# Banks of the row maxima in two kinds: diagonal tiles of four heads with one mask product, and the tiles left of the diagonal without a mask

## The reference

```python
s1 = einsum('bhtd,bhsd->bhts', q1, k1) * scale + mask     # mask: -inf right of the diagonal
s2 = einsum('bhtd,bhsd->bhts', q2, k2) * scale + mask
a1, a2 = softmax(s1), softmax(s2)
out = einsum('bhts,bhsd->bhtd', a1 - lam * a2, v)         # then a norm, Wo, residual, layer norm
```

## Time and profile before

| | |
|---|---|
| median of 3 runs | 824.52 us |
| runs | 827.38, 824.46, 824.52 us |
| profiled execution, its own time | 826.78 us |
| its span in the trace | 825.1 us |
| mean granted TensorE clock | 0.956 of full speed |
| steps of batch 0, 1, 2, 3 (first score on PE) | from about 69, 204, 362, 513 us |
| routed experts | from about 671 us to the end |

### The profile page before, as it was taken

The page is one execution under the profiler, slowest core; times in us unless marked ns, Lnnn a source line. Parts: engine busy times, 40 slices in busy tenths (PEclk is TensorE's granted clock), DMA queues, the critical chain, the costliest instruction groups (busy, mean ns, idle before and its releaser), DMA issues.

```text
span 825.1 us, 11250 instructions
## 1 busy us (share of the span) xinstructions
PE 740.3 (90%) x3890; PEld 407.1 (49%) x3890; DVE 471.5 (57%) x1040; ACT 316.6 (38%) x584; POOL 308.1 (37%) x263
## 2 busy tenths in 40 slices
PE   7588899999889999997899997899999798999993
PEld 3233334334334444543444444444326557999993
DVE  2756886763657876446678754576525342334332
ACT  2415544444555334355553331655663011111110
POOL 4057711120984131139721210321420034666653
PEclk9878999999989999999999998799999999999997
DMA  4598085102009510120282104500110056777630
GB/s 132 146 340 168 18 187 83 19 22 40 1 26 183 87 35 27 21 46 24 48 159 45 58 0 84 160 2 0 36 49 1 26 193 213 267 267 243 234 123 1
DMA packets 55831, 78.73 MB, mean 95 GB/s; under 512 B 11543, under 2 KB 43037, under 8 KB 53920
## 3 DMA queue, kind: packets, MB, share of 16 engines
q1 hardware_dynamic: 47072, 65.02, 30.8%
q0 software_dynamic: 3824, 6.83, 2.5%
q10 hardware_dynamic: 4880, 6.16, 2.2%
HBM read 58.32 MB, written 22.41 MB: 98 GB/s over the span
## 4 chain that ended last, share of the span: by engine, by line
PE 69%; DVE 13%; POOL 6%; issue 5%; DMA 3%; ACT 2%; SPq 1%; POOLq 0%; DVEq 0%; ACTq 0%
PE pv_ps L1017 16%; PE wide_ps L1097 10%; PE s_ps L856 7%; PE wide_ps L1003 7%; DVE mneg L1435 6%; PE wide_ps L844 5%; PE wide_ps L987 3%; PE s_ps L888 3%; PE s_ps L857 3%; PE wide_ps L959 3%; PE misc L1108 2%; PE pv_ps L1108 2%; PE misc L934 2%; POOL w_exp L1348 2%; PE wide_ps L992 2%
## 5 line engine op out<-in xcount | busy, mean ns | idle before, releaser
L1435 DVE TENSOR_REDUCE mneg<-s_ps 128x1 f32<-128x384 f32 (+3 forms) x352 | 215.5, 638 | 96.3 <-PE s_ps L857 92.5
L1216 ACT ACTIVATE w_exp<-wide_ps 128x512 f32<-128x512 f32 x320 | 178.9, 601 | 102.7 <-PE wide_ps L1003 101.2
L1017 PE MATMUL pv_ps<-w_exp,work 128*64 128x512 f32 x640 | 176.7, 633 | 3.0 <-ACT work L1234 1.9
L1348 POOL TENSOR_SCALAR_AFFINE_SELECT w_exp<-w_exp 128x1024 f32<-128x1024 f32 x64 | 70.7, 1108 | 278.8 <-ACT w_exp L1216 278.8
L856 PE MATMUL s_ps<-w_exp 96*128 96x256 bf16 (+3 forms) x512 | 129.9, 313 | 17.5 <-DVE mneg L1435 9.4
L1003 PE MATMUL wide_ps<-w_exp 98*128 98x512 bf16 x320 | 122.4, 397 | 15.4 <-ACT w_exp L1216 14.0
L1003 PEld LDWEIGHTS wide_ps<-w_exp 98*128 98x128 bf16 x320 | 31.0, 102 | 154.0 <-ACT w_exp L1216 83.3
L857 PE MATMUL s_ps<-mask,identb 128*128 128x128 bf16 (+2 forms) x352 | 89.1, 253 | 0.0
L1097 PE MATMUL wide_ps<-tables,w_exp 128*128 128x128 f32 x736 | 85.9, 275 | 0.0
L1097 PEld LDWEIGHTS wide_ps<-tables,w_exp 128*128 128x128 f32 x736 | 84.1, 192 | 0.1
L856 PEld LDWEIGHTS s_ps<-w_exp 96*128 96x128 bf16 x512 | 45.1, 100 | 62.9 <-DVE mneg L1435 37.2
(11 more groups left out here) (161 smaller groups left out, 962.4 us busy)
## 6 DMA issues: line engine op xcount, KB each, us to landing
w_exp<-w_up_in SPq DMA_DIRECT2D x23, 1024.0 KB, 5.5
w_exp<-q_parts SPq DMA_DIRECT2D x96, 128.0 KB, 5.1
slot_tokens<-x ACTq DMA_DIRECT2D x1, 4864.0 KB, 19.1
work<-x_in SPq DMA_DIRECT2D x8, 512.0 KB, 4.4
w_exp<-w_down_in SPq DMA_DIRECT2D x8, 512.0 KB, 8.7
q_parts<-w_exp SPq DMA_DIRECT2D x6, 512.0 KB, 6.4
w_exp<-k_parts SPq DMA_DIRECT2D x18, 128.0 KB, 4.1
gated_rows<-work SPq DMA_DIRECT2D x4, 512.0 KB, 3.0
```

What stands on the lines that cost most here:

```text
L1017: last = nc.tensor.matmul(pv_ps[s * 64:(s + 1) * 64, :], vo[:, kt, g, :], probs[:, n % NP, s, :], start=(kt == 0), stop=(kt == qt))
L1216: nc.scalar.activation(probs[:, n % NP, s], st_bank(v), ACT.Exp, scale=float(DH) ** -0.5).then_inc(st_done, 1)
L1348: nc.gpsimd.affine_select(out=e, in_=e, compare_op=ALU.is_ge, fill=0.0, base=0, pattern=[[0, 8], [1, P]], channel_multiplier=-1).then_inc( ...
L1435: nc.vector.tensor_reduce(out=mneg[:, qt, rows[0]:rows[-1] + 1], in_=s_ps[:, (v - 1) % 2, 0:len(rows) * w].rearrange("p (r k) -> p r k", r ...
```

## The change

Banks are of two kinds now. For each query tile there are first 8 diagonal banks: the diagonal key tile alone, 4 heads of 128 columns, and one mask product over all 512 columns. For query tiles 1 to 3 the key tiles left of the diagonal follow in banks of their own, without a mask: 4 heads of 128 columns, 2 heads of 256, or 1 head of 384. That is 8, 16, 24 and 40 banks, again 88 a batch. A batch has 32 mask products of 512 columns in place of 88 (of 512, 256 and 128 columns), and 224 score matmuls in place of 128. The two partial (negated) maxima of a head meet in one minimum of 128x32 on DVE after the last bank of query tiles 1 to 3, before the split, each instruction of this chain waiting for the one before. The steps over which banks are spread are unchanged.

```diff
 def banks(qt):
-    per = max(1, QT // (qt + 1))
-    return [list(range(i, i + per)) for i in range(0, HS, per)]
+    per = QT // qt if qt else HS
+    return [(True, list(range(i, i + QT))) for i in range(0, HS, QT)] + ([(False, list(range(i, i + per))) for i in range(0, HS, per)] if qt else [])
...
-        mneg = sb("mneg", [P, QT, HS])
+        mneg = sb("mneg", [P, 2, 2, HS])
...
-                rows = banks(qt)[i]
-                w = (qt + 1) * P
+                own, rows = banks(qt)[i]
                 keys = k_stack[:, b % 2]
+                tiles = slice(qt, qt + 1) if own else slice(0, qt)
+                w = (tiles.stop - tiles.start) * P
                 o = s_ps[:, (v - 1) % 2, 0:len(rows) * w].rearrange("p (n k) -> p n k", k=w)
                 for n, hs in enumerate(rows):
-                    nc.tensor.matmul(o[:, n], q_stack[0:KROWS, qt, hs, :], keys[0:KROWS, hs // 4, 0:qt + 1, :], start=(n == 0), stop=False)
-                last = nc.tensor.matmul(o[:, :, w - P:w], identb[:], mask[:].unsqueeze(1).to_broadcast([P, len(rows), P]), start=False, stop=True)
+                    last = nc.tensor.matmul(o[:, n], q_stack[0:KROWS, qt, hs, :], keys[0:KROWS, hs // 4, tiles, :], start=(n == 0),
+                                            stop=(not own and n == len(rows) - 1))
+                if own:
+                    last = nc.tensor.matmul(o, identb[:], mask[:].unsqueeze(1).to_broadcast([P, len(rows), P]), start=False, stop=True)
...
-                w = (qt + 1) * P
-                nc.vector.tensor_reduce(out=mneg[:, qt, rows[0]:rows[-1] + 1],
+                w = P if own else qt * P
+                nc.vector.tensor_reduce(out=mneg[:, 1 - own, qt % 2, rows[0]:rows[-1] + 1],
...
                     dve.wait_ge(bank_done, v)
-                    c.link(nc.vector.tensor_copy(msplit[:, qt % 2, 0:HS], mneg[:, qt]))
-                    nc.vector.tensor_tensor(msplit[:, qt % 2, HS:2 * HS], mneg[:, qt], msplit[:, qt % 2, 0:HS],
+                    if qt > 0:
+                        c.link(nc.vector.tensor_tensor(mneg[:, 0, qt % 2], mneg[:, 0, qt % 2], mneg[:, 1, qt % 2], ALU.min))
+                    c.link(nc.vector.tensor_copy(msplit[:, qt % 2, 0:HS], mneg[:, 0, qt % 2]))
+                    nc.vector.tensor_tensor(msplit[:, qt % 2, HS:2 * HS], mneg[:, 0, qt % 2], msplit[:, qt % 2, 0:HS],
                                             ALU.subtract).then_inc(split_done, 1)
```

## The result

The changed kernel took 834.65 us (median of 9 runs, 827.21 to 836.99), the kernel before, timed beside it, 824.24 (median of 9, 821.89 to 827.38): ratio 1.0105, 95% interval 1.0069 to 1.014. It is slower by 1%, ten microseconds, and lies above the range that was given. The profiled execution took 835.86 us, with a span of 834.1 against 825.1, at a mean granted clock of 0.947 against 0.956.

A forecast was written before the change was run, and what follows sets the result against it. The prediction took the kernel as PE-bound (TensorE 90% busy) with short holes around the banks. Its terms summed to -2.9 us, from 824.52 to a predicted median of 821.6 us, range 816 to 829.

The forecast's parts named there:

- the wait at step 19: Batches 1 to 3: PE waits for reduction, minimum and split after a second bank; +0.8, +0.8, +1.6, in all +3.2 us.
- +-3.4 us that I don't put in the sum: Clock, 204.7:271.9: moved banks may remove or shift a half-speed stretch; +-3.4 us, left out of the sum.
- the end of step 8: Batch 0: last reduction 0.13 us longer and the minimum adds 0.22, so +0.35 at the split of tile 2.
- tile 3's denser banks: Batch 0, steps 9 to 17: 3 or 4 banks a step become 4 or 5; +1.4 us.
- Columns: PE, all batches: same columns, 224 mask products fewer and 384 scores more; -0.1 us a batch, -0.4 in all.
- the rival of 847: All 128-column scores: weight loads set their pace, 23 us more, 847 us; chance 0.03.
- Tile 2 ahead: Steps 28 to 38: fewer three-bank clusters, so fewer PE holes; -2.3 us in batch 0, -1.3 each in batches 1 and 2.
- Tile 2 in batch 0: Batch 0, steps 0 to 8: holes between banks fall from 3.3 to 0.8 us; taken as -2.0.
- Early banks: Batches 1 and 2, steps 2 to 19: diagonal banks fill PE's idle time, later steps shrink; -1.75 us each, -3.5.
- Tile 3 in batch 3: Batch 3, steps 2 to 19: no gain from early banks, and a new cluster of three at step 6 costs 0.4 us.
- x2 behind more reductions: Steps 10 and 15, three batches: the normalised rows x2 start later behind extra reductions on DVE; +1.2 and +0.9 us.
- the drain: Slower rival, step 19: PE waits 1.57 us in each of three batches, with other costs; 830 us, chance 0.14.

The follow-up runs named there:

- E5: Changed kernel with POOL's select of step 20 cut to one of its eight blocks: 828.27 us, ratio 1.0045 to the kernel before.
- E2: Changed kernel without the minimum, so the maxima of the left tiles are not used: 831.25 us, ratio 1.0067 to the kernel before.
- E3: Kernel before with one bank of query tile 3 moved from step 18 to step 19, which then holds two: 832.13 us, ratio 1.0089.
- E1: Changed kernel with one of step 19's two banks moved back to step 18: 825.79 us, ratio 0.9999 to the kernel before.
- E9: Changed kernel with one bank moved from step 19 to 18 and tile 2's transpose in batch 0 from step 8's end to mid-step 9: 823.79 us, ratio 0.9977.
- E4: Kernel before with a minimum of a tile with itself added before the split for query tiles 1 to 3: 827.09 us, ratio 1.0025.
- E8: Kernel before with two bank kinds for tile 2 alone, its batch 0 transpose moved from step 8's end to mid-step 9: 821.07 us, ratio 0.996.
- E10: Changed kernel with both transposes later: tile 2's to mid-step 9 (batch 0), tile 3's to mid-step 20 (batches 1 to 3): 834.01 us, ratio 1.0103.

## Why the prediction was wrong

The forecast was 821.6 and the time 834.65. The step that failed is the wait at step 19, "1.57 in each of three batches", summed as +3.2. The mechanism and the place were right, and so was the sign; the size was not. It measured 2.4 of lost time in each batch (7.2), and 1.9 more in steps 20 and 21 of batches 1 and 2 with their half-speed clock, where 1.6 was to come back: 9.1 for a term of 3.2. Two things were missing in it.
- The sequence of the earlier trace rows was taken as the price: instructions of 0.18 and 0.19 us. At step 19 POOL's select of step 20 starts at just that time, and the first of DVE's small instructions behind its start is held until the select ends: 1.05 in place of 0.19. E5 (0.25 with a short select), E2 and E3 (the cast caught in its place) show it. The select was in the trace of before at the same point of the step, and it held a DVE instruction even there: x2, 0.40 in the changed kernel's batch 1, took 1.17. The forecast never asked what POOL would be doing when the split moved there.
- The forecast gave back half of each drain because PE waits for DVE behind it anyway. That wait did go, but PE then ran a stretch at half speed: 8.6 us became 9.5 and 9.6. E3 shows the same stretches at the same places in the kernel before, E1 and E5 none. At full clock (E5, and E2 in batch 1) the two steps take 8.0, so 0.6 comes back, near the 0.8 forecast, and half speed takes 1.5. The clock was named in the prediction, as "+-3.4 us that I don't put in the sum"; a wait of 2.3 us made by the change itself is a reason to put it in on one side.

Both show in E5, which has neither: its step 19 takes 5.3 us, 1.6 more than before in each batch, and 0.6 comes back in batches 1 and 2. That is 3.6 in all, and the forecast's +3.2 was nearly right for a chain without POOL beside it. The trace of before, batch 1, step 20:

```profile
272.72 1.09 POOL L1348 TENSOR_SCALAR_AFFINE_SELECT w_exp<-w_exp 128x1024 f32<-128x1024 f32 x1
272.79 1.17 DVE L1506 TENSOR_SCALAR x<-y,mv,rstd 128x256 f32<-128x256 f32 x1 [0.47 <-POOL rstd L1328]
```

The second miss is the end of step 8, forecast at +0.35 with the minimum: steps 8 to 17 of batch 0 took 6.6 more, against +1.4 for tile 3's denser banks and that. The wait for the split grew by 2.25 (3.43 against 1.18), the half-speed stretch behind it is 6.8 us long, which costs up to 3.4, and about 1 us is left for the banks. Steps 10 to 17, behind the drain, took 26.2 before, 27.0 in the changed kernel at a clock of 0.97, and 26.7 in E9 at full clock. So the denser clusters cost about 0.5 there; what they cost in step 9 can't be told from the drain, and the forecast's 1.4 was for both.

The Trainium skill, "SBUF — State Buffer", section "Who interferes with whom", has the rule that the forecast lacked: a DVE instruction with two inputs in SBUF, or a copy or cast in a mode with two ports, shares a port with GpSimd, and the one that starts second is blocked until the first is done; reductions are never blocked. The traces agree: the minimum and the subtraction (two SBUF inputs) and the cast end 0.04 to 0.05 behind POOL's instruction when they start while it runs, the subtraction keeps its 0.19 when it starts 0.03 ahead (E4), and E9's reductions keep their 0.69. Which mode the cast ran in, no run shows. By it the minimum at step 19 would have been priced at the select's 1.09 in place of its own 0.19, an estimated 0.9 more a batch, 2.7 in all.

The other terms, in the prediction's order:
- Columns, -0.4, and the loads' pace: four 128-column scores with their loads took 0.22 us from start to start, as forecast, so the rival of 847 falls, and with it the 838 estimated from the Trainium skill, "TensorE: Matmul & The Clock Gate", section "Back-to-back issue gap", with its 81 ns a pair.
- Tile 2 ahead, -2.3 in batch 0 and -1.3 each in batches 1 and 2: measured -1.8, -1.3, -1.3 over steps 28 to 36. Right but for 0.5 in batch 0, and E8, which has only tile 2's banks in two kinds, shows the same.
- Tile 2 in batch 0, -2.0: -0.8 up to step 7, then the drain.
- Early banks, -1.75 each in batches 1 and 2: batch 1 -1.4 (+0.7 and -2.1). The way differs from the forecast. PE's 3.45 us for an exponential did not shrink to 1.8: PE now meets the third bank of a cluster there, and waits 2.96 for a reduction that stands on DVE behind x2, which POOL's product holds for 2.09 (timeline after, below). Batch 2 shows +1.7 in the changed kernel, with a clock of 0.84 in its steps 7 to 18 against 0.91; in E9 it shows -1.0.
- Tile 3 in batch 3, no gain and +0.4 for step 6: steps 0 to 18 took 1.0 more. Steps 0 to 6 alone took 24.1 in place of 21.7, steps 7 to 18 34.1 in place of 35.5. The work moved forward as forecast, but into a stretch whose clock is 0.81 (0.77 before), while the steps that lost it stand at 1.00.
- x2 behind more reductions, +2.1: not seen. PE's waits for x2 fell from 7.4 to 2.8 us, and the 2.11 of the earlier trace rows to 0.4, while those of the score matmuls for a buffer rose from 9.4 to 18.0.

```profile
228.43 2.17 POOL L586 TENSOR_TENSOR w_exp<-w_exp 128x1024 f32<-128x1024 f32 x1
228.66 2.09 DVE L1511 TENSOR_SCALAR x<-y,mv,rstd 128x256 f32<-128x256 f32 x1
231.27 0.50 PE L857 MATMUL s_ps<-w_exp 96*128 96x384 bf16 x1 [2.96 <-DVE mneg L1438]
```

Among the rivals the drain had the right mechanism, with a chance of 0.14 and a time of 830; it was short by the two parts above. Had the prediction's sum been made with the measured drain (9.1 for 3.2) and the measured steps 8 to 17 (6.6 for about 1.8), it would have stood at -2.9 + 5.9 + 4.8 = +7.8, against the +9.0 of the profiled span.

What stays open: what decides whether a half-speed stretch follows a wait. The length alone does not. At step 19 the wait is the same in batches 1, 2 and 3, and half speed followed in batches 1 and 2 but not 3 of the changed kernel (2.27) and of E3 (1.93), and in batches 2 and 3 but not 1 of E2 (2.04). It followed E10's pair of waits in all three (1.00 and 1.34, in batch 3 2.0 and 0.3), none of the waits of 1.47 in E5, and not the one of 2.19 in E8. And E9 against E8 doesn't tell whether tile 3 in two kinds costs a microsecond or two.

## What to carry to other kernels

When an edit moves the last piece of work ahead of a hand-over (last bank, split, transpose), price the whole chain at its new place, with what every other engine is doing at that moment, and not from the same chain elsewhere. A spread "evenly, whatever the number" hides such moves: here a second bank in one step was worth 1% of the kernel, and one bank moved a step earlier brought it back (ratio 0.9999, interval 0.9969 to 1.0029). Look at which buffer the late task writes before moving it later.

## What the runs showed of the hardware that had not been expected

- A DVE instruction of 0.19 us on 128x32 took 1.05 beside a POOL select (1.09) and 2.08 beside a POOL product (2.12) if it started 0.08 to 0.10 behind it, and 0.19 if it started 0.03 ahead (E4). Reductions out of PSUM kept their length: of the 352 in the changed kernel's trace 114 start while a POOL instruction of over 0.9 us is running, and all of them take 0.54 to 0.69.
- A lost 2 us of PE can cost more than 2 us: behind the drains of batches 1 and 2 steps 20 and 21 took 9.5 and 9.6 us at a clock of 0.82, in place of 8.0 at 1.00 behind the shorter waits of E5. Behind the same drain in batch 3 the clock did not fall.
